# GNN layer in f32r splits on one core: x second on ScalarE's queue, layer norm in halves, a shorter warm-up on a constant

## The chip, the cores and the metric

One NeuronCore of one Trainium2 chip. The metric is the device time of one execution in microseconds, median of several runs. The kernel has one launch and all its arithmetic is on the chip.

## The reference, cut to what matters

```python
N, D, L = 4096, 128, 3
def conv(x, a, eps, W, b):
    ax = a @ x                       # a: 4096 x 4096, x: 4096 x 128
    h = ax + (1.0 + eps[0]) * ax
    for i in range(L):
        h = relu(h @ W[i].T + b[i])
    return h
h1 = maximum(layernorm(x, axis=-1), 0.0)          # eps 1e-5
out1 = conv(h1, adj, eps1, W1, b1)
out2 = conv(x2, adj, eps2, W2, b2)
return x + concatenate((out1, out2), axis=1) @ Wm.T + bm
```

All tensors are f32. Both branches multiply the same adj (64 MB), which is read once.

## The kernel before, in words

Everything is held transposed: a result is 128 features by 512 nodes (a chunk; there are 8). adj is read in units of 128 partitions x 2048 elements (1 MB): four blocks of 128 nodes, each 128 x 512, of one chunk. A unit is named (u, c): u of 8 along the summed nodes, c the chunk.

Precision comes from splitting f32 into two f32r parts. ACT copies a unit to adj_hi (`high_of_unit`, `high_of_opening`, `piece_high`), DVE subtracts it from the raw unit to give adj_lo (`low_of_opening`, `piece_low`); the features are split in the same way, the low part on POOL (`low_of_x`, `low_of_x2`). A product is three f32r matmuls: lo x hi, hi x hi, hi x lo. Branch 1 (b = 1, `first`) uses x2; branch 0 (`late`) uses the normalised and rectified x.

The chunks 0 and 1 are done together in an opening that is written out by hand, with banks acc and second_acc (`OPENING` is the order of its units). For the units (0,0) and (0,1), its numbers s = 0 and 1, which come first:
- Unit (0,0) is loaded as four transfers of one block each (adj_first, lines 211 and 336), unit (0,1) as two transfers of two blocks (adj_second, line 211). `PIECES` says so. Two queues issue transfers: SP's and ACT's. Before the first of them is needed, PE runs `WARM_UP` bf16 matmuls on a tile of zeros (line 706), which DVE fills (line 481).
- `raw_aggregate` (line 590) multiplies branch 1 in plain f32, x2_rows by adj_raw, block by block as the pieces land. A raw block shows as two records in the trace.
- Meanwhile x is normalised: DVE makes statistics (`variances`, lines 442 to 447), ACT the root (`std_of_x`, line 320), DVE the scale and the shift (`scale_and_shift`, lines 453 to 458), ACT rectifies the four blocks (`rectify`, line 327) and copies them to feat_hi (line 330), POOL makes feat_lo (line 249).
- `pieces_aggregate` then does branch 0 for both units: per unit four matmuls each of feat_hi x adj_hi, feat_hi x adj_lo and feat_lo x adj_hi (line 576).

Behind them come the opening units 2 and 3, (1,0) and (1,1), by `passes_aggregate`, then the rest of the opening and, from chunk 2 on, loops with a ring of four units. Each engine works through a list in program order; semaphores named `..._made`, `..._loaded`, `..._used` tie the lists together. A wait blocks all that follows on its engine. A ring slot is loaded again by SP once its low part is made and, for the first two, once the raw matmuls are done (`raw_used`). Layers and the merge of a chunk are set between the units of the next one.

The issue order of the opening transfers before:

```python
load_x2(0)                                   # SP
for s, i in ((0, 1), (0, 3), (1, 0), (1, 1)):  # SP: block 1, block 3, halves of (0,1)
for i in (0, 2):                             # ACT: block 0, block 2
act.dma_start(x_rows[:, 0], x_tiles[0])      # ACT: x
```

Of the kernel before, what the change touches and what calls it, by code (L numbers as in the profile page):

```python
# [6 lines left out]
def gnn_layer_kernel(nc, adj_tiles, adj_first, adj_second, x_tiles, x2_tiles, x_t, w_t, bias_t, eps, out_t):  # L7
# [5 lines left out]
    ACT = mybir.ActivationFunctionType  # L13
# [4 lines left out]
    CW = 512  # L18
# [16 lines left out]
    PIECES = ((1, 1, 1, 1), (2, 2))  # L35
    X_SLOTS = 4
    WARM_UP = 9
# [31 lines left out]
    with ExitStack() as ctx:  # L69
# [34 lines left out]
        zeros = sb("zeros", [P, CW], mybir.dt.bfloat16)  # L104
# [28 lines left out]
        zeros_made = sem("zeros_made")  # L133
# [7 lines left out]
        relu_made = sem("relu_made")  # L141
        feat2_hi_made = sem("feat2_hi_made")
# [47 lines left out]
        def _(sp):  # L190
# [18 lines left out]
            for s, i in ((0, 1), (0, 3), (1, 0), (1, 1)):  # L209
                to, piece_of, done = piece_load(s, i)  # L210
                sp.dma_start(to, piece_of).then_inc(done, 16)
# [57 lines left out]
        def _(act):  # L269
# [51 lines left out]

            def rectify(u):
# [11 lines left out]
            for i in (0, 2):  # L334
                to, piece_of, done = piece_load(0, i)
                act.dma_start(to, piece_of).then_inc(done, 16)
            act.dma_start(x_rows[:, 0], x_tiles[0]).then_inc(x_loaded[0], 16)
            act.wait_ge(zeros_made, 1)
            nc.scalar.activation(root_of_zero[:, :], zeros[:, 0:1], ACT.Sqrt)

            for i in range(len(PIECES[0])):
                piece_high(0, i)
            std_of_x(0)
            piece_high(1, 0)
            rectify(0)
            piece_high(1, 1)
            for u in range(1, U - 2):
                high_of_x2(u)
                if u > 1:
                    std_of_x(u)  # L350
                high_of_opening(2 * u)
                if u == 1:
                    std_of_x(u)
                high_of_opening(2 * u + 1)
                rectify(u)
                if u == 1:
                    high_of_x2(0)
# [47 lines left out]
        def _(dve):  # L405
# [75 lines left out]
            nc.vector.memset(zeros[:, :], 0.0).then_inc(zeros_made, 1)  # L481
# [9 lines left out]
            variances(1)  # L491
            low_of_opening(2)
            scale_and_shift(1)
# [60 lines left out]
        def _(pe):  # L554
# [39 lines left out]
            def pieces_aggregate(s):  # L594

                u, c = OPENING[s]
                out = opening_bank(c, late)
                pe.wait_ge(feat1_hi_made, u + 1)
                pe.wait_ge(hi_made, s + 1)
                passes(out, s, late, [(feat_hi, adj_hi)], start=True)  # L600
                pe.wait_ge(lo_made, s + 1)
                passes(out, s, late, [(feat_hi, adj_lo)])
                pe.wait_ge(feat1_lo_made, u + 1)
                signal(u, late, passes(out, s, late, [(feat_lo, adj_hi)]))
# [99 lines left out]
            pe.wait_ge(zeros_made, 1)  # L704
# [90 lines left out]
```

## Time and profile before

| | |
|---|---|
| median of 3 runs | 407.24 us (407.14 to 407.27) |
| the profiled execution | 407.24 us, span 405.3 us |
| PE busy | 400.6 us (99%) |
| ACT busy | 219.3 us (54%) |
| DVE busy | 218.4 us (54%) |
| POOL busy | 31.6 us (8%) |
| HBM read, written | 73.93 MB, 2.10 MB |
| granted TensorE clock over the run | 0.999 |

The span is the stretch from the first to the last instruction that the profiler saw; the time of a run also has what lies around it. Times in the rows count from the span's start. PE is the matmul engine, PEld its weight loads, SPq and ACTq the DMA issues of SyncE and ScalarE. A matmul's busy time runs past the start of the next one, since they are pipelined. The trace shows x_rows for both x_rows and x2_rows, and feat_hi for both branches.

### The profile page before, as it was taken

Reading aid. Unit: us, or ns where it says so; the run is one execution under the profiler, and the core shown is the slowest. Engines: PE = TensorE matmul, PEld = TensorE weight load, DVE = VectorE, ACT = ScalarE, POOL = GpSimd, SP = SyncE. Lnnn points to the kernel's source line nnn. Section 1 sums busy time; section 2 is a strip of 40 time slices with the busy share of each in tenths; the row PEclk is TensorE's granted clock in tenths of the full one; section 3 lists DMA queues with packets and bytes.
Section 4 is the critical chain, followed back from the end, with each engine's and each line's share of the span. In section 5 each row is a group of like instructions: output and inputs, shape, how many; then the busy total and the mean of one; then the engine's idle time right before and its main releaser. Section 6 shows DMA issues by size and latency. Waiting matters only on the chain.

```text
span 405.3 us, 4822 instructions
## 1 busy us (share of the span) xinstructions
PE 400.6 (99%) x1752; PEld 326.0 (80%) x1752; DVE 218.4 (54%) x258; ACT 219.3 (54%) x257; POOL 31.6 (8%) x35
## 2 busy tenths in 40 slices
PE   8999999999999999999999999999999999999997
PEld 3688888888888888888888888888888888888886
DVE  3898887656364434551645517345373444755223
ACT  4896667657564533555433556334565335766034
POOL 0343332100010000000100001000000000000100
PEclk9999999999999999999999999999999999999999
DMA  8997786764636175234574336653175551840100
GB/s 304 421 378 295 298 299 236 249 205 158 232 142 209 44 240 207 107 119 192 177 288 167 122 125 228 238 207 142 65 264 202 207 194 40 271 169 2 52 0 27
DMA packets 14029, 76.21 MB, mean 188 GB/s; under 512 B 1920, under 2 KB 2176, under 8 KB 6080
## 3 DMA queue, kind: packets, MB, share of 16 engines
q1 hardware_dynamic: 12240, 71.18, 47.3%
q0 software_dynamic: 1200, 3.93, 2.9%
q10 hardware_dynamic: 576, 0.92, 0.6%
q8 instruction: 9, 0.15, 0.2%
q14 instruction: 4, 0.03, 0.0%
HBM read 73.93 MB, written 2.10 MB: 188 GB/s over the span
## 4 chain that ended last, share of the span: by engine, by line
PE 96%; DMA 1%; DVE 1%; ACT 1%; ACTq 0%; issue 0%; DVEq 0%
PE acc L558 24%; PE acc L562 24%; PE acc L559 24%; PE second_acc L562 3%; PE second_acc L559 3%; PE second_acc L558 3%; PE hidden L559 3%; PE hidden L558 3%; PE hidden L562 3%; PE acc L576 2%; PE second_acc L576 2%; DMA x_rows<-x_tiles 1%; PE merged L559 1%; PE merged L558 1%; PE merged L562 1%; ACT x_rows L327 0%
## 5 line engine op out<-in xcount | busy, mean ns | idle before, releaser
L558 PE MATMUL acc<-adj_hi,feat_lo 128*128 128x512 f32 x432 | 168.7, 390 | 0.0
L562 PE MATMUL acc<-adj_lo,feat_hi 128*128 128x512 f32 x432 | 168.6, 390 | 0.0
L559 PE MATMUL acc<-adj_hi,feat_hi 128*128 128x512 f32 x432 | 168.0, 389 | 0.0
L418 DVE TENSOR_TENSOR adj_lo<-adj_raw,adj_hi 128x2048 fp32r<-128x2048 f32 x48 | 108.3, 2288 | 37.3 <-ACT adj_hi L273 36.4
L273 ACT ACTIVATE adj_hi<-adj_raw 128x2048 fp32r<-128x2048 f32 x48 | 90.4, 1928 | 17.1 <-PE acc L562 15.2
L424 DVE TENSOR_TENSOR act_lo<-act_f,act_hi 128x512 fp32r<-128x512 f32 x60 | 41.0, 690 | 105.5 <-ACT act_f L293 105.5
L562 PEld LDWEIGHTS acc<-adj_lo,feat_hi 128*128 128x128 f32 x432 | 81.1, 188 | 17.5
L559 PEld LDWEIGHTS acc<-adj_hi,feat_hi 128*128 128x128 f32 x432 | 81.2, 188 | 17.2
L558 PEld LDWEIGHTS acc<-adj_hi,feat_lo 128*128 128x128 f32 x432 | 81.1, 188 | 17.1
L292 ACT ACTIVATE act_hi<-hidden,bias 128x512 fp32r<-128x512 f32 x45 | 30.9, 686 | 96.3 <-PE hidden L562 96.3
L478 DVE TENSOR_TENSOR adj_lo<-adj_raw,adj_hi 128x2048 fp32r<-128x2048 f32 x14 | 31.6, 2290 | 6.2 <-ACT adj_hi L311 6.2
L292 ACT ACTIVATE act_hi<-acc,ax_scale 128x512 fp32r<-128x512 f32 x13 | 8.9, 688 | 46.2 <-PE acc L562 43.1
L293 ACT ACTIVATE act_f<-hidden,bias 128x512 f32<-128x512 f32 x45 | 30.9, 688 | 0.0
L311 ACT ACTIVATE adj_hi<-adj_raw 128x2048 fp32r<-128x2048 f32 x14 | 26.1, 1901 | 0.0
L263 POOL DMA_DIRECT2D out_t<-y_sb x7 | 3.8, 545 | 281.6 <-DVE y_sb L436 281.6
L558 PE MATMUL second_acc<-adj_hi,feat_lo 128*128 128x512 f32 x48 | 18.7, 389 | 0.0
L562 PE MATMUL second_acc<-adj_lo,feat_hi 128*128 128x512 f32 x48 | 18.7, 389 | 0.0
L559 PE MATMUL second_acc<-adj_hi,feat_hi 128*128 128x512 f32 x48 | 18.7, 389 | 0.0
L559 PE MATMUL hidden<-act_hi,w_hi 128*128 128x512 f32 x45 | 17.7, 393 | 0.0
L558 PE MATMUL hidden<-act_hi,w_lo 128*128 128x512 f32 x45 | 17.6, 391 | 0.0
L562 PE MATMUL hidden<-act_lo,w_hi 128*128 128x512 f32 x45 | 17.6, 390 | 0.0
L436 DVE SCALAR_TENSOR_TENSOR y_sb<-merged,bias,x_res 128x512 f32<-128x512 f32 x7 | 5.2, 749 | 22.0 <-PE merged L562 22.0
(80 smaller groups left out, 248.4 us busy)
## 6 DMA issues: line engine op xcount, KB each, us to landing
adj_raw<-adj_tiles SPq DMA_DIRECT2D x62, 1024.0 KB, 5.0
x_rows<-x_tiles SPq DMA_DIRECT2D x15, 256.0 KB, 6.7
x_res<-x_t POOLq DMA_DIRECT2D x8, 256.0 KB, 6.6
out_t<-y_sb POOLq DMA_DIRECT2D x7, 256.0 KB, 2.3
adj_raw<-adj_second SPq DMA_DIRECT2D x2, 512.0 KB, 6.9
adj_raw<-adj_first ACTq DMA_DIRECT2D x2, 256.0 KB, 3.9
adj_raw<-adj_first SPq DMA_DIRECT2D x2, 256.0 KB, 4.9
w_raw<-w_t SPq DMA_DIRECT2D x1, 512.0 KB, 5.9
```

Source lines behind the costliest of these rows:

```text
L273: nc.scalar.activation(adj_hi[:, u % RING, :], adj_raw[:, u % RING, :], ACT.Copy).then_inc(hi_made, 1)
L292: nc.scalar.activation(act_hi[:, b, :], src[:, :], **how).then_inc(act_hi_made[b], 1)
L293: nc.scalar.activation(act_f[:, b, :], src[:, :], **how).then_inc(act_f_made[b], 1)
L311: nc.scalar.activation(adj_hi[:, s % RING, :], adj_raw[:, s % RING, :], ACT.Copy).then_inc(hi_made, 1)
L418: nc.vector.tensor_tensor(adj_lo[:, u % RING, :], adj_raw[:, u % RING, :], f32(adj_hi[:, u % RING, :]), ALU.subtract).then_inc(lo_made, 1)
L424: nc.vector.tensor_tensor(act_lo[:, b, :], act_f[:, b, :], f32(act_hi[:, b, :]), ALU.subtract).then_inc(act_lo_made[b], 1)
L436: nc.vector.scalar_tensor_tensor(y_sb[:, :], merged[:, :], bias[:, MATS - 2:MATS - 1], x_res[:, :], ALU.add, ALU.add).then_inc(y_made, 1)
L478: nc.vector.tensor_tensor(adj_lo[:, s % RING, :], adj_raw[:, s % RING, :], f32(adj_hi[:, s % RING, :]), ALU.subtract).then_inc(lo_made, 1)
L558: nc.tensor.matmul(out, lhs_lo, rhs_hi, start=start, stop=False)
L559: nc.tensor.matmul(out, lhs_hi, rhs_hi, start=False, stop=False)
L562: return nc.tensor.matmul(out, lhs_hi, rhs_lo, start=False, stop=stop)
L576: last = nc.tensor.matmul(out[:, :], feat[:, b, u * JB + j, :], adj[:, slot, cols], start=start and k == 0 and j == 0, stop=False)
```

## The change

Four things:
- ACT's queue issues block 0, x, block 3; SP's queue issues x2, block 1, block 2 and the halves of unit (0,1). Before, ACT had block 0, block 2, x and SP x2, block 1, block 3 and the halves.
- The warm-up has 8 matmuls instead of 9 and reads a constant of ones that exists before the engines' lists start; the tile of zeros shrinks to one column, for the table load alone.
- The rectified x of node unit 0 is made in two halves of two blocks (`rectify_half`), with the copy of the second half of unit (0,1) between them, and PE takes it in halves (`norm_aggregate` in place of `pieces_aggregate`).
- ACT makes std of unit 0 ahead of the copy of block 3. For unit 1 it copies opening unit 2 in two halves with std between them, and DVE makes the scale of unit 1 ahead of the low part of opening unit 2.

The diff:

```diff
--- before.py
+++ after.py
@@ -33,8 +33,10 @@
 
 
     PIECES = ((1, 1, 1, 1), (2, 2))
+    SECOND_UNIT = len(PIECES[0]) - 1
     X_SLOTS = 4
-    WARM_UP = 9
+    WARM_UP = 8
+    HALF = JB // 2
 
 
 
@@ -101,7 +103,7 @@
         eps_sb = sb("eps_sb", [P, 2])
         ax_scale = sb("ax_scale", [P, 2])
         root_of_zero = sb("root_of_zero", [P, 1])
-        zeros = sb("zeros", [P, CW], mybir.dt.bfloat16)
+        zero = sb("zero", [P, 1])
 
         act_f = sb("act_f", [P, 2, CW])
         act_hi = sb("act_hi", [P, 2, CW], F32R)
@@ -130,7 +132,7 @@
         lo_made = sem("lo_made")
         fine_hi_made = sem("fine_hi_made")
         fine_lo_made = sem("fine_lo_made")
-        zeros_made = sem("zeros_made")
+        zero_made = sem("zero_made")
         unit_used = sem("unit_used")
         raw_used = sem("raw_used")
         stats_step = sem("stats_step")
@@ -139,6 +141,8 @@
         rstd_made = sem("rstd_made")
         feat1_hi_made = sem("feat1_hi_made")
         relu_made = sem("relu_made")
+        half_relu_made = sem("half_relu_made")
+        half_feat1_made = sem("half_feat1_made")
         feat2_hi_made = sem("feat2_hi_made")
         feat1_lo_made = sem("feat1_lo_made")
         feat2_lo_made = sem("feat2_lo_made")
@@ -206,7 +210,7 @@
 
 
             load_x2(0)
-            for s, i in ((0, 1), (0, 3), (1, 0), (1, 1)):
+            for s, i in ((0, 1), (0, 2), (1, 0), (1, 1)):
                 to, piece_of, done = piece_load(s, i)
                 sp.dma_start(to, piece_of).then_inc(done, 16)
             for s, (u, c) in enumerate(OPENING):
@@ -319,6 +323,25 @@
                 act.wait_ge(var_made, u + 1)
                 nc.scalar.activation(std[:, :], var_eps[:, :], ACT.Sqrt).then_inc(std_made, 1)
 
+            def high_of_half(s, h):
+
+                cols = slice(h * HALF * CW, (h + 1) * HALF * CW)
+                if h == 0:
+                    act.wait_ge(raw_loaded[s], 16)
+                last = nc.scalar.activation(adj_hi[:, s, cols], adj_raw[:, s, cols], ACT.Copy)
+                if h == 1:
+                    last.then_inc(hi_made, 1)
+
+            def rectify_half(h, rectified, rounded):
+
+                blocks = slice(h * HALF, (h + 1) * HALF)
+                for j in range(blocks.start, blocks.stop):
+                    xs = x_rows[:, 0, j, :]
+                    last = nc.scalar.activation(xs, xs, ACT.Relu, bias=shift[:, j:j + 1], scale=rstd[:, j:j + 1])
+                last.then_inc(rectified, 1)
+                act.wait_ge(rectified, 1)
+                nc.scalar.activation(feat_hi[:, 0, blocks, :], x_rows[:, 0, blocks, :], ACT.Copy).then_inc(rounded, 1)
+
             def rectify(u):
 
                 act.wait_ge(rstd_made, u + 1)
@@ -331,30 +354,36 @@
                                      ACT.Copy).then_inc(feat1_hi_made, 1)
 
 
-            for i in (0, 2):
+            for i in (0, 3):
+                if i == 3:
+                    act.dma_start(x_rows[:, 0], x_tiles[0]).then_inc(x_loaded[0], 16)
                 to, piece_of, done = piece_load(0, i)
                 act.dma_start(to, piece_of).then_inc(done, 16)
-            act.dma_start(x_rows[:, 0], x_tiles[0]).then_inc(x_loaded[0], 16)
-            act.wait_ge(zeros_made, 1)
-            nc.scalar.activation(root_of_zero[:, :], zeros[:, 0:1], ACT.Sqrt)
-
-            for i in range(len(PIECES[0])):
+            act.wait_ge(zero_made, 1)
+            nc.scalar.activation(root_of_zero[:, :], zero[:, :], ACT.Sqrt)
+
+            for i in range(len(PIECES[0]) - 1):
                 piece_high(0, i)
             std_of_x(0)
+            piece_high(0, len(PIECES[0]) - 1)
             piece_high(1, 0)
-            rectify(0)
+            act.wait_ge(rstd_made, 1)
+            rectify_half(0, half_relu_made, half_feat1_made)
             piece_high(1, 1)
-            for u in range(1, U - 2):
+            rectify_half(1, relu_made, feat1_hi_made)
+            high_of_x2(1)
+            high_of_half(2, 0)
+            std_of_x(1)
+            high_of_half(2, 1)
+            high_of_opening(3)
+            rectify(1)
+            high_of_x2(0)
+            for u in range(2, U - 2):
                 high_of_x2(u)
-                if u > 1:
-                    std_of_x(u)
+                std_of_x(u)
                 high_of_opening(2 * u)
-                if u == 1:
-                    std_of_x(u)
                 high_of_opening(2 * u + 1)
                 rectify(u)
-                if u == 1:
-                    high_of_x2(0)
             for u in (U - 2, U - 1):
                 high_of_x2(u)
                 std_of_x(u)
@@ -478,7 +507,7 @@
                 nc.vector.tensor_tensor(adj_lo[:, s % RING, :], adj_raw[:, s % RING, :], f32(adj_hi[:, s % RING, :]),
                                         ALU.subtract).then_inc(lo_made, 1)
 
-            nc.vector.memset(zeros[:, :], 0.0).then_inc(zeros_made, 1)
+            nc.vector.memset(zero[:, :], 0.0).then_inc(zero_made, 1)
 
             for i in range(2):
                 piece_low(0, i)
@@ -489,8 +518,8 @@
             for i in range(len(PIECES[1])):
                 piece_low(1, i)
             variances(1)
+            scale_and_shift(1)
             low_of_opening(2)
-            scale_and_shift(1)
             low_of_opening(3)
             for u in range(2, U - 2):
                 variances(u)
@@ -591,17 +620,26 @@
                                                 start=(j == 0), stop=False)
                 last.then_inc(raw_used, 1)
 
-            def pieces_aggregate(s):
-
-                u, c = OPENING[s]
-                out = opening_bank(c, late)
-                pe.wait_ge(feat1_hi_made, u + 1)
-                pe.wait_ge(hi_made, s + 1)
-                passes(out, s, late, [(feat_hi, adj_hi)], start=True)
-                pe.wait_ge(lo_made, s + 1)
-                passes(out, s, late, [(feat_hi, adj_lo)])
-                pe.wait_ge(feat1_lo_made, u + 1)
-                signal(u, late, passes(out, s, late, [(feat_lo, adj_hi)]))
+            def norm_aggregate():
+
+                for h in range(2):
+                    pe.wait_ge(feat1_hi_made if h else half_feat1_made, 1)
+                    for s in range(2):
+                        out = opening_bank(s, late)
+                        whole = s == 0 or h == 1
+                        pe.wait_ge(hi_made if whole else fine_hi_made, s + 1 if whole else SECOND_UNIT + 1)
+                        for j in range(h * HALF, (h + 1) * HALF):
+                            slot, cols = columns(s, j)
+                            nc.tensor.matmul(out[:, :], feat_hi[:, late, j, :], adj_hi[:, slot, cols],
+                                             start=(j == 0), stop=False)
+                        pe.wait_ge(lo_made if whole else fine_lo_made, s + 1 if whole else SECOND_UNIT + 1)
+                        for j in range(h * HALF, (h + 1) * HALF):
+                            slot, cols = columns(s, j)
+                            nc.tensor.matmul(out[:, :], feat_hi[:, late, j, :], adj_lo[:, slot, cols],
+                                             start=False, stop=False)
+                pe.wait_ge(feat1_lo_made, 1)
+                for s in range(2):
+                    signal(0, late, passes(opening_bank(s, late), s, late, [(feat_lo, adj_hi)]))
 
             def passes_aggregate(s, b):
 
@@ -701,13 +739,12 @@
                 nc.tensor.matmul(merged_pair[q // 2][:, at:at + QUARTER], w_raw[:, 2 * LAYERS + late, :],
                                  act_f[:, late, quarter(q)], start=False, stop=(q % 2 == 1)).then_inc(quarter_done[q], 1)
 
-            pe.wait_ge(zeros_made, 1)
+            ones = nc.const_aps.tensor(1.0, [P, CW], mybir.dt.bfloat16)
             for _ in range(WARM_UP):
-                nc.tensor.matmul(merged[:, :], zeros[:, 0:P], zeros[:, :], start=True, stop=True)
+                nc.tensor.matmul(merged[:, :], ones[:, 0:P], ones[:, :], start=True, stop=True)
             for at in range(len(PIECES)):
                 raw_aggregate(at)
-            for at in range(len(PIECES)):
-                pieces_aggregate(at)
+            norm_aggregate()
             for b in BRANCH_ORDER:
                 for at in (2, 3):
                     passes_aggregate(at, b)
```

How the lists move. First ACT, from its first transfer to the copies of x2; before (feat_hi<-x_rows is the normalised x, feat_hi<-x2_rows the other branch):

```order
L336 DMA adj_raw<-adj_first 128x512 x2
L337 DMA x_rows<-x_tiles 128x512
L339 ACT_TABLE_LOAD
L339 ACTIVATE root_of_zero<-zeros 128x1
L304 ACTIVATE adj_hi<-adj_raw 128x512 x4
L320 ACTIVATE std<-var_eps 128x4
L304 ACTIVATE adj_hi<-adj_raw 128x1024
L327 ACTIVATE x_rows<-x_rows,shift,rstd 128x128 x4
L330 ACTIVATE feat_hi<-x_rows 128x512
L304 ACTIVATE adj_hi<-adj_raw 128x1024
L315 ACTIVATE feat_hi<-x2_rows 128x512
```

And the same place of ACT in the changed kernel, behind its table load:

```order
L308 ACTIVATE adj_hi<-adj_raw 128x512 x3
L324 ACTIVATE std<-var_eps 128x4
L308 ACTIVATE adj_hi<-adj_raw 128x512
L308 ACTIVATE adj_hi<-adj_raw 128x1024
L340 ACTIVATE x_rows<-x_rows,shift,rstd 128x128 x2
L343 ACTIVATE feat_hi<-x_rows 128x256
L308 ACTIVATE adj_hi<-adj_raw 128x1024
L340 ACTIVATE x_rows<-x_rows,shift,rstd 128x128 x2
L343 ACTIVATE feat_hi<-x_rows 128x256
L319 ACTIVATE feat_hi<-x2_rows 128x512
```

The root moved ahead of the copy of block 3, and the rectification became two halves around the copy of unit (0,1)'s second half. Next PE, from the warm-up to the end of branch 0's work on node unit 0 (acc1 and second_acc1 are the banks of branch 1); before:

```order
L706 MATMUL merged<-zeros 128x512 x9
L590 MATMUL acc1<-adj_raw,x2_rows 128x512 x4
L590 MATMUL second_acc1<-adj_raw,x2_rows 128x512 x4
L576 MATMUL acc0<-adj_hi,feat_hi 128x512 x4
L576 MATMUL acc0<-adj_lo,feat_hi 128x512 x4
L576 MATMUL acc0<-adj_hi,feat_lo 128x512 x4
L576 MATMUL second_acc0<-adj_hi,feat_hi 128x512 x4
L576 MATMUL second_acc0<-adj_lo,feat_hi 128x512 x4
L576 MATMUL second_acc0<-adj_hi,feat_lo 128x512 x4
```

And the same place of PE in the changed kernel:

```order
L744 MATMUL merged<-const-bfloat16-1.0 128x512 x8
L619 MATMUL acc1<-adj_raw,x2_rows 128x512 x4
L619 MATMUL second_acc1<-adj_raw,x2_rows 128x512 x4
L633 MATMUL acc0<-adj_hi,feat_hi 128x512 x2
L638 MATMUL acc0<-adj_lo,feat_hi 128x512 x2
L633 MATMUL second_acc0<-adj_hi,feat_hi 128x512 x2
L638 MATMUL second_acc0<-adj_lo,feat_hi 128x512 x2
L633 MATMUL acc0<-adj_hi,feat_hi 128x512 x2
L638 MATMUL acc0<-adj_lo,feat_hi 128x512 x2
L633 MATMUL second_acc0<-adj_hi,feat_hi 128x512 x2
L638 MATMUL second_acc0<-adj_lo,feat_hi 128x512 x2
L605 MATMUL acc0<-adj_hi,feat_lo 128x512 x4
```

The same 24 matmuls of branch 0 stand in another order: both units' first halves, both units' second halves, and feat_lo last for both.

## Rows read from the trace of the kernel before

**Rows 1.** The page's chain that ended last, shares of the span by engine.

```profile
PE 96%; DMA 1%; DVE 1%; ACT 1%; ACTq 0%; issue 0%; DVEq 0%
```

**Rows 2.** Waits of PEld, 12.9 to 406 us: who for whom, us in total, times, longest.

```profile
PEld acc L576 <- ACT feat_hi L330: 1.1, 1, 1.1
```

**Rows 3.** Windows: length; busy of PE, PEld, DVE, ACT, POOL; granted clock, DMA share, GB/s.

```profile
5.26:12.93 7.67, 7.28 (x18) 2.78 (x16) 5.90 (x19) 5.26 (x11) 0.00 (x0) 1.00 1.04 414
12.93:29.54 16.61, 16.61 (x73) 13.78 (x74) 14.93 (x33) 14.48 (x21) 7.09 (x5) 1.00 1.00 406
```

**Rows 4.** Timeline, 1 to 15 us, warm-up to norm: start, us, engine, line, operation.

```profile
1.12 0.27 DVE L481 MEMSET zeros<- 128x256 uint32 x1 [1.12 <-PEq L789]
...
1.45 3.99 PE L706 MATMUL merged<-zeros 128*128 128x512 bf16 x9 [1.45 <-DVE zeros L481]
...
5.26 3.61 PE L590 MATMUL acc<-adj_raw,x_rows 128*128 128x512 f32 x8
...
7.62 0.41 PEld L590 LDWEIGHTS acc<-adj_raw,x_rows 128*128 128x128 f32 x2 [0.45 <-DMA adj_raw<-adj_first]
...
8.96 0.30 PEld L590 LDWEIGHTS second_acc<-adj_raw,x_rows 128*128 128x128 f32 x2 [0.93 <-issue]
9.00 3.67 PE L590 MATMUL second_acc<-adj_raw,x_rows 128*128 128x512 f32 x8
...
12.93 1.19 PE L576 MATMUL acc<-adj_hi,feat_hi 128*128 128x512 f32 x4 [0.26 <-ACT feat_hi L330]
...
13.96 1.08 PE L576 MATMUL acc<-adj_lo,feat_hi 128*128 128x512 f32 x4
```

**Rows 5.** The chain that ended last in order of time, 0 to 50 us.

```profile
1.93 5.85 DMA x_rows<-x_tiles
7.80 0.88 DVE stats L442 x4
...
10.56 1.66 ACT x_rows L327 x4
12.24 0.64 ACT feat_hi L330
```

**Rows 6.** SP's issues, then transfers in order of issue: KB, us from issue to landing.

```profile
1.45 0.90 SPq L211 DMA_DIRECT2D adj_raw<-adj_first  x2
2.39 0.96 SPq L211 DMA_DIRECT2D adj_raw<-adj_second  x2
...
x_rows<-x_tiles SPq DMA_DIRECT2D x1, 256.0 KB, 3.2
adj_raw<-adj_first ACTq DMA_DIRECT2D x1, 256.0 KB, 3.4
...
adj_raw<-adj_first ACTq DMA_DIRECT2D x1, 256.0 KB, 4.3
adj_raw<-adj_first SPq DMA_DIRECT2D x1, 256.0 KB, 4.1
...
adj_raw<-adj_first SPq DMA_DIRECT2D x1, 256.0 KB, 5.7
...
adj_raw<-adj_second SPq DMA_DIRECT2D x1, 512.0 KB, 6.5
...
adj_raw<-adj_second SPq DMA_DIRECT2D x1, 512.0 KB, 7.3
```

**Rows 7.** Timeline of ACT, 4 to 13 us.

```profile
9.33 0.20 ACT L320 ACTIVATE std<-var_eps 128x4 f32<-128x4 f32 x1 [1.09 <-DVE var_eps L447]
...
12.78 1.04 ACT L304 ACTIVATE adj_hi<-adj_raw 128x1024 fp32r<-128x1024 f32 x1
```

**Rows 8.** Timeline of DVE and POOL, 10 to 19 us.

```profile
10.45 2.43 DVE L470 TENSOR_TENSOR adj_lo<-adj_raw,adj_hi 128x512 fp32r<-128x512 f32 x3
...
12.96 1.29 POOL L249 TENSOR_TENSOR feat_lo<-x_rows,feat_hi 128x512 fp32r<-128x512 f32 x1 [12.26 <-ACT feat_hi L330]
...
16.64 2.29 DVE L478 TENSOR_TENSOR adj_lo<-adj_raw,adj_hi 128x2048 fp32r<-128x2048 f32 x1
```

## The prediction

> **What bounds the kernel now.** I read the chain of waits first. It lies on the TensorE (PE) for 96% of the span, and the few per cent that are not PE hold one transfer of x and some steps of DVE and ACT [rows 1]. Second, the waits of PE's weight loads after 12.9 us: in 393 us there is a single one, on the first feat_hi [rows 2]. So from 12.93 us to the end PE is the bound and has no stall that an edit of ACT, DVE or a queue could give back. The windows by stage say the same: PE is busy 16.61 of 16.61 us behind 12.93, but 7.28 of 7.67 us in the stage before it, at a granted clock of 1.00 in both [rows 3]. What the change can move is therefore the moment at which the dense part of PE starts, and the rest of the kernel follows as a block.
>
> Third, PE in order of time [rows 4]. DVE fills zeros, then nine warm-up matmuls run from 1.45 us; they stand 0.43 us apart (3.99 us less the drain of the last, by nine). Eight raw records per group follow, two for each adj block (f32), also 0.43 us apart: a block costs 0.86. PE waits at 7.62 for block 3 of unit (0,0) and at 8.96 for the first half of unit (0,1). The last group starts at 9.00 and could be followed at 12.50: its busy time ends at 12.67, and in this group of rows a matmul's busy time reaches some 0.16 us past the start of its successor. PE starts its norm matmuls only at 12.93, and these four take 1.03 us to the next group at 13.96, whereas four f32r matmuls at the steady pace of 0.227 take 0.91 (16.61 us for 73 records [rows 3]). So the dense part has an effective start of 13.96 - 0.91 = 13.05. Between 12.50 and 13.05 lie **0.55 us, all that the norm chain costs now**.
>
> Fourth, that chain in order of time [rows 5]: x is issued at 1.93, lands at 7.78, statistics at 7.80, rectification at 10.56 (1.66 us for four blocks), feat_hi at 12.24 for 0.64 us.
>
> Fifth, the landings of the opening transfers [rows 6], as issue plus time to landing. On the SP queue: x2 1.00 + 3.2 = 4.2; block 1 1.45 + 4.1 = 5.6; block 3 1.9 + 5.7 = 7.6; halves of unit (0,1) 2.39 + 6.5 = 8.9 and 2.9 + 7.3 = 10.2. On the ACT queue: block 0 1.00 + 3.4 = 4.4; block 2 1.45 + 4.3 = 5.75; x at 7.78. The first two places of both queues land in pairs, 4.2 and 4.4, then 5.6 and 5.75, and the third ones at 7.6 and 7.78. The three places on ACT and the first three on SP hold 256 KB each, of one shape in SBUF.
>
> **The change, part by part.**
>
> *The places of the transfers.* The tensors trade places between queues, the sizes at each place stay. I let each place keep its landing: x lands at 5.75 instead of 7.78, **block 2 at 7.58 instead of 5.75** (third on SP, where block 3 stood), block 3 at 7.78 instead of 7.58 (third on ACT). Unit (0,1) stays at 8.9 and 10.2. The bounds for block 2 are 5.75 (its own landing before) and 8.9 (the next landing on SP); I take 7.58, because the row is one of the same queue, place and size.
>
> *Warm-up.* One matmul of 0.43 goes, and PE no longer waits for DVE's zeros (memset 1.12 to 1.39), so it starts somewhere between 1.00, when the queues of the same engines start, and 1.45. Eight matmuls end between 4.4 and 4.9 us, and both block 0 and x2 have landed by 4.4. PE gets to the raw work 0.4 to 0.8 us earlier. This is worth **nothing**, for block 1 lands at 5.6 and ends at about 6.5, and then PE must wait for block 2 until 7.58. The cover is that landing; without it the whole 0.4 to 0.8 would still be cut by unit (0,1)'s landings at 8.9 and 10.2.
>
> *Raw stage.* At 7.6 PE has two blocks done where it had three. Behind it stand blocks 2 and 3 and four blocks of unit (0,1), twelve records: 12 x 0.429 = 5.15, and 0.08 for restarting after a wait (3.67 us for the last group, where eight records and a drain of 0.16 make 3.59). 7.64 + 5.15 + 0.08 = **12.87 us** instead of 12.50, a loss of 0.37. No landing stops it on the way, since block 3 is there at 7.78 for 8.5, and unit (0,1) at 8.9 and 10.2 for 9.4 and 11.2.
>
> *Norm in halves.* DVE gets to the statistics once the low part of block 1 is done, at about 7.0 (landing 5.57, 0.64 copy, 0.7 subtract) instead of 7.80. From there to std it takes 1.53 (7.80 to 9.33 [rows 5, 7]): 8.55. ACT then copies block 3 (0.64) and the first half of unit (0,1) (1.04 [rows 7]) until 10.4; the scale is ready at about 9.8 (1.23 behind std), under that cover. A half of the rectification is two of four instructions, 0.83 to 0.9; the half copy was never timed and lies between 0.32 (half of 0.64) and 0.64; with 0.64 the first half is ready by 11.9. PE asks for it at 12.87. So the norm's **0.55 us goes whole**: PE runs from the last raw matmul into the first norm matmul without a gap. ACT goes on with the second half of unit (0,1) (1.04, to 12.9) and the second half of the norm, ready by 14.4 at the latest; PE asks for it after eight matmuls, 12.87 + 1.82 = 14.69. POOL's low part takes 1.29 [rows 8], to 15.7; PE asks at 12.87 + 16 x 0.227 = 16.5. The same twenty-four matmuls run in another order, at no price. On DVE the three low parts that took 2.43 behind the scale [rows 8] start 0.8 earlier and are not late.
>
> *Later units.* ACT splits the copy of opening unit 2 around std, and DVE puts the scale of unit 1 ahead of the 2.29 us low part [rows 8]. That makes this low part end at about 19.2 to 19.4 instead of 18.93; PE, which has it third in its order, asks at 12.87 + 24 x 0.227 + 8 x 0.227 = 20.1. Hidden, with 0.7 us to spare. One transfer, the one behind lo_made of that unit, is issued up to 0.5 us later and has ten us to its use.
>
> **The sum**: the effective start moves from 13.05 to 12.87, that is **-0.18 us** (-0.55 of norm, +0.37 of raw stage). The profiled execution took 407.24 us in all with a span of 405.3, and the median of the runs is 407.24 too, so 407.24 - 0.18 = **407.06 us**. A difference of 0.2%, 0.8 us, is about what a measurement can tell from no change; this is far inside.
>
> A rule bears on the wait ahead of block 2. The row shows a granted clock of 1.00 through the raw stage [rows 3] though PE waited twice in it [rows 4], 0.2 to 0.3 us each; now it waits once, about 1 us. The Trainium skill (TensorE: Matmul & The Clock Gate, section "HAM oscillation — how this bites in real kernels") says that waits for DMA between bursts of matmuls can bring the throttled clock back. The trace has no wait so long in this stage and can't say. By the row the sum stays -0.18; by the rule it becomes rival 2.
>
> **Rivals.**
> 1. *Block 2 lands early.* Its transfer meets other traffic than block 3 did. If it is there by 6.6, PE goes on until unit (0,1) lands, as now; the raw stage ends at 12.50 and the whole norm gap is won: 407.24 - 0.55 = 406.7. Against it: every place's landing followed its neighbour on the other queue within 0.2 us.
> 2. *The clock.* The warm-up matmuls, one pass over 512 columns, are 0.43 apart, and the f32r ones later 0.227: 1.2 and 2.4 GHz. The raw records begin as the nine warm-ups end. With a shorter warm-up and then a wait, the low level may still hold when block 2 arrives. A raw record is then 0.86. Blocks 0 and 1 would end at 4.55 + 4 x 0.86 = 8.0, 0.35 later than block 2 needs; each further low record costs 0.43. It turns slower than before by over 0.8 from the second such record (0.35 + 0.86 - 0.18 = 1.03). If the low level holds for blocks 2 and 3, four records, the time is 407.06 + 0.35 + 1.72 = **409.1**, slower. For it: there is one warm-up matmul fewer, and a wait where there was work. Against: PE's work from the first warm-up to the end of block 1 is 5 us unbroken, longer than the 3.8 us ahead of the first raw record. The same skill page, section "What's actually happening", says that the clock starts throttled and activity releases it, which allows both.
> 3. *The second half of the norm is late*: one slow step of ACT or DVE eats the 0.3 us of slack, PE waits up to 0.6. 407.1 to 407.7.
> 4. *x is not earlier by its new place* (the queues share unevenly): x at 7.78 as before. The chain is then that of before, std 9.33, blocks to 11.1, first half at 12.6, still in time, the second late by 0.4: 407.5.
>
> **How the numbers follow.** Forecast 0.58; rival 1 0.22; rival 2 0.08; rival 3 0.05; rival 4 0.04; 0.03 for a gain above 0.8, which needs transfers to land earlier too (with today's landings PE can't end the raw stage before 8.9 + 1.72 + 1.72 = 12.3, a gain of 0.7). Same: 0.58 + 0.22 + 0.05 + 0.04 = 0.89; slower 0.08; faster 0.03. The range goes from rival 1 with 0.1 for the measurement, 406.6, to the forecast with a low clock until block 2 (0.35) and a landing 0.2 later, 407.6.
>
> **What would show it.** Right: PE waits about 1 us for an adj_first transfer that lands near 7.6; x lands near 5.8; no wait of PE on feat_hi; the first norm matmul starts at 12.9 with four in 0.91. Wrong: block 2 before 7 us (rival 1), raw records 0.86 apart behind 7.6 (rival 2), a wait on the second feat_hi or on feat_lo (rivals 3, 4), or any wait of PE behind 20 us.

## The result and the profile after

The changed kernel takes **406.39 us** (median of 16 runs, 406.11 to 406.64), the kernel before in the same comparison 407.28 us (median of 16, 406.86 to 408.61). The ratio is 0.9976, with a 95% interval of 0.9969 to 0.9983: 0.9 us faster, and outside the forecast range of 406.6 to 407.6. The profiled execution took 406.39 us with a span of 404.7, against 407.24 and 405.3.

The page's busy times, and its chain by engine, of the changed kernel:

```profile
PE 400.2 (99%) x1751; PEld 325.4 (80%) x1751; DVE 219.1 (54%) x258; ACT 219.4 (54%) x259; POOL 30.5 (8%) x35
...
PE 97%; DMA 2%; ACTq 0%; DVE 0%; issue 0%; DVEq 0%
```

PE is the bound as before [rows 1], and the norm chain of DVE and ACT has left the path: their part is 0. The landings of the opening's transfers, in the form of [rows 6] (KB, us from issue to landing; issues at 1.00, 1.45, 1.9, 2.4 and 2.9 us as before):

```profile
x_rows<-x_tiles SPq DMA_DIRECT2D x1, 256.0 KB, 3.5
adj_raw<-adj_first ACTq DMA_DIRECT2D x1, 256.0 KB, 3.6
...
x_rows<-x_tiles ACTq DMA_DIRECT2D x1, 256.0 KB, 4.6
adj_raw<-adj_first SPq DMA_DIRECT2D x1, 256.0 KB, 4.4
...
adj_raw<-adj_first SPq DMA_DIRECT2D x1, 256.0 KB, 5.1
adj_raw<-adj_first ACTq DMA_DIRECT2D x1, 256.0 KB, 6.3
```

x lands at 6.0, block 2 at 7.0, block 3 at 8.3. PE's weight loads from the opening to unit 3, whose idle times show the waits (against [rows 4] and [rows 2]):

```profile
4.75 0.30 PEld L619 LDWEIGHTS acc<-adj_raw,x_rows 128*128 128x128 f32 x2 [1.05 <-DMA x_rows<-x_tiles]
5.86 0.30 PEld L619 LDWEIGHTS acc<-adj_raw,x_rows 128*128 128x128 f32 x2 [0.82 <-DMA adj_raw<-adj_first]
7.02 0.30 PEld L619 LDWEIGHTS acc<-adj_raw,x_rows 128*128 128x128 f32 x2 [0.86 <-DMA adj_raw<-adj_first]
8.31 0.30 PEld L619 LDWEIGHTS acc<-adj_raw,x_rows 128*128 128x128 f32 x2 [0.99 <-DMA adj_raw<-adj_first]
8.84 0.19 PEld L619 LDWEIGHTS second_acc<-adj_raw,x_rows 128*128 128x128 f32 x1 [0.24 <-issue]
...
17.96 0.87 PEld L605 LDWEIGHTS acc<-adj_hi,feat_hi 128*128 128x128 f32 x4
18.86 0.87 PEld L605 LDWEIGHTS acc<-adj_hi,feat_lo 128*128 128x128 f32 x4
20.04 0.77 PEld L605 LDWEIGHTS acc<-adj_lo,feat_hi 128*128 128x128 f32 x4 [0.31 <-DVE adj_lo L507]
...
23.62 0.87 PEld L605 LDWEIGHTS acc<-adj_hi,feat_hi 128*128 128x128 f32 x4
```

The same two marks in the kernel before, the first load for opening unit 2 and the one twenty-four matmuls behind it:

```profile
18.28 0.87 PEld L576 LDWEIGHTS acc<-adj_hi,feat_hi 128*128 128x128 f32 x4
...
23.72 0.87 PEld L576 LDWEIGHTS acc<-adj_hi,feat_hi 128*128 128x128 f32 x4
```

Every raw block of unit (0,0) now waits for a transfer, and the norm follows without a wait on feat_hi. Unit 2 is reached at 17.96 instead of 18.28: 0.32 us are won in the opening. Then there is a new wait of 0.31 for the low part of unit 2, and by the next mark only 0.10 us are left. At that point the profile shows less than the forecast of 0.18. The rest of the gain is made where I had not looked: between the first and the last weight load of the merges (product of act_hi with w_lo; count, durations, first to last start). Before and after:

```profile
L558 PEld LDWEIGHTS merged<-act_hi,w_lo x15: 187/187/188, 109.6 to 397.5; 128*128 128x128 f32 x15
```

```profile
L587 PEld LDWEIGHTS merged<-act_hi,w_lo x15: 187/188/188, 109.4 to 396.9; 128*128 128x128 f32 x15
```

287.9 us before, 287.5 after, for the same matmuls without a wait in either. PE's weight loads behind a layer show how. Before, from the first load to the eleventh after it:

```profile
210.77 0.19 PEld L558 LDWEIGHTS acc<-adj_hi,feat_lo 128*128 128x128 f32 x1
...
213.31 0.19 PEld L562 LDWEIGHTS acc<-adj_lo,feat_hi 128*128 128x128 f32 x1
```

and after:

```profile
210.46 0.19 PEld L587 LDWEIGHTS acc<-adj_hi,feat_lo 128*128 128x128 f32 x1
...
212.96 0.19 PEld L591 LDWEIGHTS acc<-adj_lo,feat_hi 128*128 128x128 f32 x1
```

Eleven steps take 2.54 us before and 2.50 after (0.231 and 0.227 each). In these stretches ACT writes act_hi and act_f and DVE act_lo; before:

```profile
210.51 0.69 ACT L292 ACTIVATE act_hi<-hidden,bias 128x512 fp32r<-128x512 f32 x1 [6.70 <-PE hidden L562]
211.10 0.68 ACT L293 ACTIVATE act_f<-hidden,bias 128x512 f32<-128x512 f32 x1
...
211.88 0.69 DVE L424 TENSOR_TENSOR act_lo<-act_f,act_hi 128x512 fp32r<-128x512 f32 x1 [5.25 <-ACT act_f L293]
```

The six layer matmuls ahead are 0.02 us slower after than before, so a layer's place is worth 0.02 net, and there are 28. From the layers' start at 78 us to the last merge the two traces drift apart by 0.54 us.

### The profile page after: what moved, and what is told of

Same layout as the page of the kernel before. It is cut to its first block, busy times and chain, and to the rows that moved or that the text cites. A ratio compares the mean times of both kernels' runs of the same rounds, so it can differ in the third digit from the quotient of the medians.

```text
span 404.7 us, 4822 instructions
## 1 busy us (share of the span) xinstructions
PE 400.2 (99%) x1751; PEld 325.4 (80%) x1751; DVE 219.1 (54%) x258; ACT 219.4 (54%) x259; POOL 30.5 (8%) x35
## 4 chain that ended last, share of the span: by engine, by line
PE 97%; DMA 2%; ACTq 0%; DVE 0%; issue 0%; DVEq 0%
PE acc L591 24%; PE acc L588 24%; PE acc L587 24%; PE second_acc L587 3%; PE second_acc L591 3%; PE second_acc L588 3%; PE hidden L588 3%; PE hidden L591 3%; PE hidden L587 3%; PE acc L605 2%; PE second_acc L605 2%; DMA adj_raw<-adj_first 2%; PE second_acc L619 1%; PE merged L588 1%; PE merged L591 1%; PE merged L587 1%
## 5 line engine op out<-in xcount | busy, mean ns | idle before, releaser
L277 ACT ACTIVATE adj_hi<-adj_raw 128x2048 fp32r<-128x2048 f32 x48 | 90.3, 1925 | 16.5 <-PE acc L591 14.6
L315 ACT ACTIVATE adj_hi<-adj_raw 128x2048 fp32r<-128x2048 f32 x13 | 24.2, 1900 | 0.0
```

The costliest lines, as they stand in the source:

```text
L277: nc.scalar.activation(adj_hi[:, u % RING, :], adj_raw[:, u % RING, :], ACT.Copy).then_inc(hi_made, 1)
L315: nc.scalar.activation(adj_hi[:, s % RING, :], adj_raw[:, s % RING, :], ACT.Copy).then_inc(hi_made, 1)
```

## The experiments

The theories, in short. A: where the act tiles lie in SBUF sets the pace of those matmuls; the change shrank the tile of zeros (1 KB) ahead of them to one column, and so moved them. B: all of the gain is made in the opening. C: the pace follows from where PE's instructions lie. D: it follows from something else in the program. Places are those that the allocator gives, in bytes within a partition.

**e1.** The kernel before with the zeros behind all other tiles.

```diff
-        zeros = sb("zeros", [P, CW], mybir.dt.bfloat16)
         act_f = sb("act_f", [P, 2, CW])
...
         y_sb = sb("y_sb", [P, CW])
+        zeros = sb("zeros", [P, CW], mybir.dt.bfloat16)
```

> The kernel before with one line moved: the 1 KB tile of zeros is allocated behind all others, so that act_f, act_hi, act_lo, x_res and y_sb lie 1 KB lower in SBUF, as in the changed kernel; the program is the same. Theory A (where the act tiles lie sets the spacing of some matmuls; the two profiles drift apart by 0.55 us between 37 and 388 us): 406.7 us, the dense part shorter by 0.5 us, no 0.229 to 0.236 us spacings behind the layers. Theory B (all of the gain is made in the opening): 407.3 us, as before. Theory C (the spacings come from where the instructions lie in the program): also 407.3, since no instruction moves.

407.51 us, ratio 1.0008 (0.9998 to 1.0017); 287.9 us from merge to merge. A, as put, fails: act tiles 1 KB lower change nothing.

**e2.** The changed kernel with 1020 unused bytes.

```diff
         zero = sb("zero", [P, 1])
+        pad = sb("pad", [P, CW // 2 - 1])
```

> The changed kernel with an unused tile of 1020 bytes ahead of act_f, so that the act tiles lie where they did before. Theory A: 406.9 us, the 0.55 us come back. Theories B and C: 406.4 us, as the changed kernel.

406.36 us, 0.997 (0.9959 to 0.9981), 287.5 us: as the changed kernel. A seems to fail again. But the allocator rounds to 32 bytes, and pad and zero together are 32 bytes more than the old zeros, so e2 did not put the act tiles where they had been, and e1 did not put them where the change does. This came out only when I listed the places: a multiple of 64 for all act tiles in the kernel before and in e1, 32 past one in the changed kernel and in e2.

**e3.** The changed kernel with the queues of before.

```diff
-            for s, i in ((0, 1), (0, 2), (1, 0), (1, 1)):
+            for s, i in ((0, 1), (0, 3), (1, 0), (1, 1)):
...
-            for i in (0, 3):
-                if i == 3:
-                    act.dma_start(x_rows[:, 0], x_tiles[0]).then_inc(x_loaded[0], 16)
+            for i in (0, 2):
                 to, piece_of, done = piece_load(0, i)
                 act.dma_start(to, piece_of).then_inc(done, 16)
+            act.dma_start(x_rows[:, 0], x_tiles[0]).then_inc(x_loaded[0], 16)
```

> The changed kernel with the queues of before (ACT: block 0, block 2, x; SP: x2, block 1, block 3). Landings by place (my prediction): block 2 near 5.8 and x near 7.8; raw stage ends at 12.5, the first half of the norm is ready at 12.4 to 12.6, the second some 0.4 late: within 0.2 us of the changed kernel, 406.2 to 406.6. Rival (the early x is what makes the norm free): 406.8 or more, with a wait of PE on feat_hi.

407.10 us, 0.9995 (0.9985 to 1.0005): the rival is right. PE's weight loads in e3, one wait each for the two halves of the norm, the copy and the low part of unit 2:

```profile
12.42 0.30 PEld L632 LDWEIGHTS acc<-adj_hi,feat_hi 128*128 128x128 f32 x2 [0.70 <-ACT feat_hi L343]
...
14.59 0.30 PEld L632 LDWEIGHTS acc<-adj_hi,feat_hi 128*128 128x128 f32 x2 [0.48 <-ACT feat_hi L343]
...
18.42 0.76 PEld L604 LDWEIGHTS acc<-adj_hi,feat_hi 128*128 128x128 f32 x4 [0.31 <-ACT adj_hi L331]
...
20.82 0.76 PEld L604 LDWEIGHTS acc<-adj_lo,feat_hi 128*128 128x128 f32 x4 [0.71 <-DVE adj_lo L506]
```

The early x is worth 0.7 us in this program. Between the two profiles 0.46 us are lost ahead of unit 2 (18.42 against 17.96) and 0.28 behind it, where ACT and DVE, with x late, come late as well. The expected 406.2 to 406.6 is missed: the halves alone do not make up for a late x.

**e4.** The changed kernel with DVE's two steps of unit 1 in the old order.

```diff
-            scale_and_shift(1)
             low_of_opening(2)
+            scale_and_shift(1)
             low_of_opening(3)
```

> The changed kernel with the low part of opening unit 2 ahead of the scale of unit 1 on DVE again, as before. In the profile of the changed kernel PE waits near 20.0 us for that low part, and the next matmuls stand 0.2 us later than the steady pace gives. If that wait is the loss: 406.2 us and no wait of PE behind 12.9. Rival (another wait takes its place, on the features of unit 1): 406.4 or more.

406.49 us, 0.9974 (0.9963 to 0.9985). The wait at 20 us stays (0.29) and another of 0.49 comes at 22.96, on the low part of unit 3. The 406.2 us are missed; another wait did take the place of the first, though not on the features of unit 1. The low part of unit 2 was not late because of the scale: its copy was late, behind std on ACT. So why was std late? e8 asks that.

**e5.** `WARM_UP = 8` in the kernel before.

> The kernel before with 8 warm-up matmuls instead of 9, nothing else. PE's list of instructions behind the warm-up begins one matmul and one weight load earlier. In the opening the 0.43 us lie ahead of a landing: nothing. Theory C (the spacing of the matmuls at the layers follows from where PE's instructions lie): the spacings of 0.229 to 0.236 us change, and with them the drift; if the pattern is that of the changed kernel, 406.8 us. Theory D (it follows from something else in the program that the change altered): pattern and time as before, 407.3 us.

407.26 us, 0.9994 (0.9986 to 1.0003), 288.0 us from merge to merge. The shorter warm-up is worth nothing by itself, and C falls.

**e6.** `WARM_UP = 9` in the changed kernel.

> The changed kernel with 9 warm-up matmuls instead of 8. The ninth ends at 4.8 us, about when x2 and block 0 are there: nothing in the opening. Theory C: the pattern of spacings changes, the mean of the dense part by up to 0.5 us in either direction. Theory D: 406.4 us with the pattern of the changed kernel.

406.23 us, 0.9968 (0.9956 to 0.998), 287.4 us. C falls here too. This profile reached unit 2 at 17.64 and had no wait there, though ACT and DVE have the order of the changed kernel (see e8); what one warm-up matmul more or less does can't be told from nothing.

**e7.** The changed kernel with unit 1 as before on ACT and DVE.

```diff
-            high_of_half(2, 0)
+            high_of_opening(2)
             std_of_x(1)
-            high_of_half(2, 1)
             high_of_opening(3)
...
-            scale_and_shift(1)
             low_of_opening(2)
+            scale_and_shift(1)
             low_of_opening(3)
```

> The changed kernel with the order of unit 1 as before, on ACT (opening unit 2 copied whole, then std) and on DVE (low part of unit 2, then the scale). If the wait near 20 us comes from std standing between the two half copies and ahead of the low part: no wait of PE behind 12.9 us, 406.15 us. Rival (the features of unit 1 become late, a wait near 24 us): 406.4 or more.

406.18 us, 0.9966 (0.9953 to 0.9979), no wait of PE behind the raw stage. As expected.

**e8.** The changed kernel with one wait more on POOL.

```diff
             for u in range(1, U):
+                if u == 1:
+                    pool.wait_ge(var_made, 2)
                 low_of_x2(u)
```

> The changed kernel with one more wait: POOL starts the low part of x2 of unit 1 only when DVE has written var_eps of unit 1. In the changed kernel that 128x4 instruction of DVE takes 1.31 us, from 15.09, the stretch in which POOL works on the low part of x2; elsewhere it takes 0.17. If POOL's work is what holds it: 0.17 us here, std at 15.4, no wait of PE near 20 us, 406.15 us. Rival (it waits for something else, the half copy's data or ACT): it stays at 1.3 us and the time at 406.4.

406.13 us, 0.9964 (0.9951 to 0.9977), and no wait near 20 us. DVE and POOL in the changed kernel:

```profile
15.09 1.31 DVE L476 TENSOR_SCALAR var_eps<-mean_var 128x4 f32<-128x4 f32 x1
...
15.09 1.29 POOL L246 TENSOR_TENSOR feat_lo<-x_rows,feat_hi 128x512 fp32r<-128x512 f32 x1
```

and in e8:

```profile
15.16 0.17 DVE L478 TENSOR_SCALAR var_eps<-mean_var 128x4 f32<-128x4 f32 x1
...
15.81 0.91 DVE L485 TENSOR_TENSOR newton<-rstd 128x4 f32<-128x4 f32 x1
...
15.40 1.30 POOL L246 TENSOR_TENSOR feat_lo<-x_rows,feat_hi 128x512 fp32r<-128x512 f32 x1 [0.20 <-DVE var_eps L478]
```

An instruction of 4 elements a partition takes 1.31 us, until POOL's subtract ends. With POOL held back it takes 0.17, and a later one of the chain, which now falls into POOL's work, takes 0.91 and ends with it; std has been made by then. POOL holding DVE is shown.

That the wait at 20 us is gone would not show it by itself. In the twelve profiles that have the norm in halves and not the wait of e8, var_eps and POOL's subtract start within 0.01 us of each other; eight times var_eps is held for 1.3 us, and four times (e6, e10, e13, e14) it takes 0.17. In e10:

```profile
14.93 0.17 DVE L477 TENSOR_SCALAR var_eps<-mean_var 128x4 f32<-128x4 f32 x1
...
15.58 0.69 DVE L484 TENSOR_TENSOR newton<-rstd 128x4 f32<-128x4 f32 x1
...
14.93 1.32 POOL L247 TENSOR_TENSOR feat_lo<-x_rows,feat_hi 128x512 fp32r<-128x512 f32 x1
```

There newton is the one held, to 16.27, when POOL ends at 16.25, and PE has no wait at unit 2. So whether the wait of 0.31 comes looks like the outcome of a race within 0.01 us. Each kernel has one profile, so no run shows whether one and the same kernel can have both outcomes, nor what decides.

The Trainium skill (SBUF — State Buffer, section "Who interferes with whom") has DVE and GpSimd share one pair of ports under an exclusive lock. The rows agree. var_eps has a single SBUF input; the same section counts `tensor_scalar`, which it is, among the operations that can enter a two-port mode and then contend, but which mode this instruction ran in no run here shows.

**e9.** The kernel before with 32 unused bytes ahead of act_f.

```diff
+        shim = sb("shim", [P, 8])
         act_f = sb("act_f", [P, 2, CW])
```

> The kernel before with an unused tile of 32 bytes a partition ahead of act_f; the program is the same. By the allocator act_f, act_hi and act_lo lie at multiples of 64 bytes in the kernel before and in e1, which both show the slow pattern, and 32 bytes past one in the changed kernel and in e2, e3, e4, e6, e7 and e8, which all show the quick one. Theory A, mended (the place within 64 bytes sets the spacing, not the place as such): the quick pattern, a drift of -0.54 us between 78 and 388 us, 406.8 us. Theory D (something else of the changed program, such as the numbers of its semaphores): the pattern and the time of before, 407.3 us.

406.74 us, 0.999 (0.9981 to 0.9998), and the quick pace:

```profile
L559 PEld LDWEIGHTS merged<-act_hi,w_lo x15: 187/188/188, 110.4 to 397.9; 128*128 128x128 f32 x15
```

287.5 us. D falls: not one instruction differs from the kernel before. The interval only just leaves out 1; the pace is the stronger evidence.

**e10.** The same shim in the changed kernel.

> The changed kernel with an unused tile of 32 bytes a partition ahead of act_f, which puts the act tiles at multiples of 64 bytes. Theory A, mended: the slow pattern of before comes back, 406.9 us. Theory D: 406.4 us with the quick pattern.

407.00 us, 0.9993 (0.9984 to 1.0002): of the changed kernel's 406.39, 0.6 us are given back. 288.0 us:

```profile
L588 PEld LDWEIGHTS merged<-act_hi,w_lo x15: 187/188/188, 109.3 to 397.3; 128*128 128x128 f32 x15
```

**e11.** The kernel before with the queues of the change (the reverse of e3's diff).

> The kernel before with the queue order of the change alone. Block 2 lands at 7.0 to 7.4 us as in the changed kernel, block 3 near 8.0, x near 5.9; the raw stage ends about 12.7 to 12.9 instead of 12.5; the whole rectification still stands in one piece behind the copies of blocks 2 and 3 and half of unit (0,1), ready at 11.9 to 12.3, ahead of that end. Dense part from 12.8 instead of 13.05 and the slow pattern: 407.0 us. Rival (the halves are needed for any gain): 407.3 or more.

406.98 us, 0.9994 (0.9985 to 1.0003). It reached unit 2 at 17.82, with one wait of 0.4 on feat_hi. Placed where it was expected; its interval still holds 1.

**e12.** e7 with the queues of before.

> The changed kernel with the queues of before and with unit 1 in the order of before: warm-up, halves of the norm and the quick pattern are left. In e3 PE waited 0.7 us for the first half, 0.5 for the second and 0.3 and 0.7 for the copies and low part of opening unit 2. With unit 1 as before the last two go: 406.4 to 406.6 us. Rival (they come back as a wait on the features of unit 1): 407.0 us.

406.51 us, 0.9982 (0.9973 to 0.9991). With unit 1 in its old order the late x costs 0.3 us (to e7's 406.18), no longer 0.7.

**e13, e14, e15.** e7 with shims of 32 bytes around one tile, so that act_hi, act_f or act_lo alone lies at a multiple of 64. The theories are F (ACT's writes of act_hi are the cause), G (act_f is) and H (DVE's writes of act_lo are). For e13:

```diff
         act_f = sb("act_f", [P, 2, CW])
+        shim0 = sb("shim0", [P, 8])
         act_hi = sb("act_hi", [P, 2, CW], F32R)
+        shim1 = sb("shim1", [P, 8])
         act_lo = sb("act_lo", [P, 2, CW], F32R)
```

> The kernel of e7 with act_hi alone at a multiple of 64 bytes (act_f and act_lo 32 past one). Theory F (the spacings behind the layers come from ACT writing act_hi): of the 0.54 us between the patterns a part comes back, 406.4 to 406.7 us, spacings of 0.236 behind the layers, and the layer matmuls themselves, which read act_hi, are quicker than 0.238. Theory G (it is act_f that is written or read by then): 406.1 us or a little less, since only the layer matmuls change.

> The kernel of e7 with act_f alone at a multiple of 64 bytes. Theory F: 406.2 us, nothing changes, since PE never reads act_f. Theory G: 406.4 to 406.7 us with spacings of 0.236 behind the layers.

> The kernel of e7 with act_lo alone at a multiple of 64 bytes. Theories F and G: 406.2 us; a third theory, H (DVE's write of act_lo holds PE), gives 406.4 us or more.

406.72, 406.69 and 407.28 us (0.9982, 0.9977 and 0.9994; intervals 0.9973 to 0.9991, 0.9968 to 0.9986, 0.9984 to 1.0003). All three lose against e7's 406.18, e15 the most. F misses e14 and e15, G misses e13 and e15. H has e15 right, but act_lo alone does not set the pace either: in the table below e10 and e15 have it at the same place, and differ by 0.4 us. So it is not one tile. Two things weaken these runs: the shims move the tiles behind them too, which counts once the period is not 64 (e16), and PE does read act_f, in the last chunk from 398 us on, behind the stretch that is compared.

**e16.** e7 with 64 unused bytes ahead of act_f.

```diff
+        shim = sb("shim", [P, 16])
         act_f = sb("act_f", [P, 2, CW])
```

> The kernel of e7 with an unused tile of 64 bytes a partition ahead of act_f: all act tiles lie 32 bytes past a multiple of 128, where e7 has them 96 past one. Theory A, mended (64 bytes): the quick pattern, 406.2 us. Theory I (128 bytes, and the quick place is 96): slower spacings behind the layers, 406.6 us or more. If it is quick, what e13 to e15 lost is the price of tiles that lie at different places within 64.

406.45 us, 0.9978 (0.9969 to 0.9987), 287.8 us: between the two paces. A period of 64 bytes is out. The time is not told apart from e7's; the pace is.

The places of the tiles and the dense part, over all profiles (each kernel profiled once; merge to merge, from the answers as above):

| act_f / act_hi / act_lo, place within 128 bytes | kernels | merge to merge, us |
|---|---|---|
| 96 / 96 / 96 | after, e2, e3, e4, e6, e7, e8, e9, e12 | 287.4 to 287.5 |
| 32 / 32 / 32 | e16 | 287.8 |
| 0 / 32 / 32 | e14 | 287.8 |
| 96 / 0 / 32 | e13 | 287.9 |
| 64 / 64 / 64 | before, e1, e5, e11 | 287.9 to 288.0 |
| 0 / 0 / 0 | e10 | 288.0 |
| 96 / 96 / 0 | e15 | 288.4 |

## Why the prediction was wrong, point by point

**The step that failed: "from 12.93 us to the end PE is the bound and has no stall", hence "the rest of the kernel follows as a block".** There is no stall, but the pace is not fixed. I took 0.227 us a matmul from one row over 16 us that lie ahead of every layer [rows 3], and never compared the pace behind the layers. The diff's line on the zeros I priced at the warm-up alone; it also moved act_f and every tile behind it, act_hi and act_lo among them. That is worth 0.54 us in the traces, 0.46 by e9 and 0.6 by e10. With this term of the sum the forecast would have been 406.5. Pairs of kernels at nearly the same pace give what is left for the opening: the changed kernel is 0.35 us below e9, both quick, and e10 0.2 below the kernel before, both slow. My 0.18 for the opening is within the noise of either, by errors that partly cancel, as the next point shows.

**The places of the transfers.** The rule that a place keeps its landing held within 0.3 us for x (6.0 against 5.75) and failed by 0.5 to 0.6 for blocks 2 and 3: 7.0 instead of 7.58 and 8.3 instead of 7.78. What ends the raw stage's waits is block 3, at 8.31, not block 2. The two errors nearly cancel: that the raw stage ended only 0.14 us from the forecast is luck. A reading was off too: at 7.62 only a weight load waited for block 3 in the kernel before, and PE was busy without a break from 5.26 to 8.87 [rows 4]; the sum does not rest on it. The reach of unit 2 was forecast 0.18 us earlier and came 0.32 earlier.

**One profile stood for the opening.** The four profiled kernels with the old queues and the whole norm reach unit 2 at 18.28 (before), 18.45 (e5), 18.58 (e1) and 19.19 (e9); mine was the quickest. The change's queues give 17.64 to 18.37 in eleven further profiles, 17.96 in its own. Middle to middle that is about 0.6 us rather than 0.32, and with 0.54 from the pace and 0.2 given back at unit 2 it makes the measured 0.9. This third part is an account of single profiles, not a separate measurement. The times speak for it: the kernel before spreads over 1.7 us in its 16 runs and the changed one over 0.5, and the profiled execution of e9, the one at 19.19, took 407.51 us where its median is 406.74.

**Norm in halves.** "The norm's 0.55 goes whole": right, no wait on feat_hi is left. e3 shows what I left out of the price of x's place: without the early x the halves save little.

**Warm-up, worth nothing**: e5 and e6 show nothing that is clear of the noise.

**Later units, "hidden, with 0.7 us to spare"**: wrong. The wait of 0.31 came where I had costed var_eps at 0.17; it took 1.31 under POOL's subtract. That it came in the profile of the change may be chance (e8), but that it could come I had not seen. A row of before with the same face, where 0.16 us is usual, lay in the timeline, and I had not asked what it was:

```profile
24.04 0.77 DVE L454 TENSOR_TENSOR newton<-rstd 128x4 f32<-128x4 f32 x1
```

**Rival 1** (block 2 early) came half true, and its price, 406.7, was nearer than my own. **Rival 2** (the clock) came in part in some profiles, at no price that can be seen. In e4 two raw records, of block 0 and block 1, are 0.85 us apart, where 0.43 is the high level's spacing:

```profile
5.69 0.34 PEld L619 LDWEIGHTS acc<-adj_raw,x_rows 128*128 128x128 f32 x1 [0.52 <-DMA adj_raw<-adj_first]
6.54 0.19 PEld L619 LDWEIGHTS acc<-adj_raw,x_rows 128*128 128x128 f32 x1 [0.51 <-issue]
7.02 0.19 PEld L619 LDWEIGHTS acc<-adj_raw,x_rows 128*128 128x128 f32 x1 [0.28 <-DMA adj_raw<-adj_first]
```

By this spacing the clock was at 1.2 GHz until about 6.5 us, though the profile's granted clock reads 1.00 there. Block 2 is there at 7.0, and PE comes to it only at 7.4, so up to 0.4 us is lost at that place; e4 still reaches unit 2 at 17.81, and what the low level cost it is not shown. In no profile did the wait for block 2, up to 1.8 us in e16, bring the low level back. The Trainium skill's warning of waits for DMA (TensorE: Matmul & The Clock Gate, section "HAM oscillation — how this bites in real kernels") did not bite at this length. **Rival 3** named the right kind of thing in the wrong place. **Rival 4** did not occur.

The quickest version by its median is e8, 406.13 us, with e7 at 406.18 and e6 at 406.23 beside it; the three are not told apart, and their intervals overlap that of the changed kernel. I did not try them together, nor places of the act tiles beyond those in the table.

## What to carry to other kernels

Where one engine is busy for 99% of the time, 400 us times a thousandth is as much as a stall in the opening: compare its pace in several stretches, not only its gaps. A diff that changes the size of a tile changes the place of all tiles behind it, so list the places of both kernels before calling the edit free, and repeat a comparison with a shim of 32 bytes before crediting the code. And look for small instructions that take several times their usual time, here 1.31 us for 0.17: another engine can hold them, and that is a wait like any other.

## What the runs showed of the hardware that was not expected

The spacing of f32r matmuls of 128x512 depends on where tiles lie that ACT and DVE write in the same stretch. Behind a layer it is 0.227 us with all act tiles at 96 of 128 bytes, and up to 0.24 at single matmuls in the kernel before (212.84 to 213.08), where they lie at 64; the layer's own six matmuls, which read the act tiles, are up to 0.24 apart at either place. It makes 0.54 us in all between the kernel's old place and its new one, and 0.9 between the worst mix and the best (288.4 against 287.5). Against the kernel before, the changed kernel and e7, nothing was changed in e9, e10 and e16 but the place of the act tiles and of the two tiles behind them, x_res and y_sb, so that place is the cause is shown; that it is the act tiles' place, and not that of these two, which PE never reads, is argued. What in the chip makes it so, which pair of accesses meets, and whether the period is 128 bytes or more, stays open. A 128x4 instruction of DVE was held for 1.1 us by a subtract on POOL (e8).
